# A four-network graph kernel on one core: edges taken from the highest destinations down, and two layers swept downward in blocks of 4, 4, 4 and 1

## What is computed

```
edge_index = stack([src, dst])
x = layernorm(x + L0(x, edge_index, edge_weight))   # three GCN layers with edge weights, then a linear layer
x = layernorm(x + L1(x, src, dst))                  # two SAGE layers: mean over the neighbours
x = layernorm(x + L2(x, edge_index))                # encoder, five GRU steps (segment_sum of m[src]), decoder
x = layernorm(x + L3(x, edge_index))                # one GCN layer with degree counts
# in every layer: out = segment_sum(h[src] * something, dst, num_segments=n)
```

## Time and profile before

| | us |
|---|---|
| three runs | 5507.01, 5510.14, 5510.31 (median 5510.14) |
| the profiled execution | 5502.16, its span in the trace 5500.3 |
| PE busy | 4752.6 (86%) |
| POOL busy | 2479.1 (45%), nearly all before 3043 us |
| DVE busy | 1804.3 (33%) |
| ACT busy | 1189.9 (22%) |
| read from HBM, written | 1160 MB, 240 MB |

### The profile page before, as it was taken

How to read it: one execution, slowest core, us unless ns; L and a number is a source line. 1 busy time by engine, 2 the same in 40 slices (tenths; PEclk the granted TensorE clock), 3 DMA queues, 4 the chain that set the end, 5 groups by cost and what they waited for, 6 DMA issues and landing times. The chain is left out here.

```text
span 5500.3 us, 77896 instructions
## 1 busy us (share of the span) xinstructions
PE 4752.6 (86%) x25659; PEld 2555.6 (46%) x25659; DVE 1804.3 (33%) x3215; ACT 1189.9 (22%) x2478; POOL 2479.1 (45%) x1704
## 2 busy tenths in 40 slices
PE   3544545599699999999999899899999999999999
PEld 3544544544244444444454444444444444444444
DVE  9999999900001000110050211302113021130642
ACT  4555555411011111111120101202102021120320
POOL 3888888878878888888888100000000000000000
PEclk7555555599899999999999999999999999999999
DMA  9999993399699999999989787585775857758477
GB/s 359 369 365 336 341 302 48 31 336 285 179 287 300 274 301 288 296 276 298 288 232 266 225 272 238 154 297 191 244 252 180 299 185 252 244 184 298 144 229 249
DMA packets 717098, 1402.13 MB, mean 255 GB/s; under 512 B 268372, under 2 KB 356264, under 8 KB 691880
## 3 DMA queue, kind: packets, MB, share of 16 engines
q1 hardware_dynamic: 477388, 1342.89, 73.0%
q0 software_dynamic: 225216, 0.70, 7.9%
q10 hardware_dynamic: 14364, 56.99, 2.7%
HBM read 1160.09 MB, written 240.25 MB: 255 GB/s over the span
## 5 line engine op out<-in xcount | busy, mean ns | idle before, releaser
L849 PE MATMUL psum<-arena 128*128 128x512 f16 (+3 forms) x14014 | 3666.9, 422 | 103.9 <-issue 51.9
L849 PEld LDWEIGHTS psum<-arena 128*128 (+2 forms) x14014 | 1668.2, 123 | 2040.4 <-issue 961.9
L556 POOL DMA_INDIRECT W_adj<-arena x782 | 1211.1, 1549 | 279.2 <-issue 259.8
L556 POOL DMA_INDIRECT C_adj<-arena x782 | 1213.5, 1552 | 238.4 <-issue 238.4
L711 POOL TENSOR_TENSOR arena<-arena 128x512 f32 (+1 forms) x13 | 21.5, 1651 | 1716.6 <-DVE arena L1247 1716.6
L433 DVE TENSOR_SCALAR_CACHE_REDUCE arena<-arena 128x2048 bf16<-128x2048 f32 (+7 forms) x392 | 709.4, 1875 | 0.0
L505 PE MATMUL psum<-arena 128*128 (+1 forms) x6664 | 225.0, 167 | 545.3 <-DVE arena L455 523.4
L505 PEld LDWEIGHTS psum<-arena 128*128 128x128 bf16 x6664 | 214.3, 104 | 560.4 <-issue 506.6
L1443 DVE COPY arena<-psum 128x512 f32<-128x512 f32 (+1 forms) x39 | 23.2, 653 | 1174.0 <-PE psum L867 1174.0
L273 ACT ACTIVATE arena<-arena 128x1024 bf16<-128x1024 f32 (+7 forms) x392 | 298.4, 773 | 453.0 <-DVE arena L433 439.0
L1445 DVE TENSOR_SCALAR arena<-psum,arena 128x512 f32<-128x512 f32 x30 | 21.9, 748 | 1038.9 <-PE psum L849 1038.9
(11 more groups left out here) (236 smaller groups left out, 2571.3 us busy)
## 6 DMA issues: line engine op xcount, KB each, us to landing
arena<-C_adj SPq DMA_DIRECT2D x784, 384.0 KB
arena<-W_adj SPq DMA_DIRECT2D x294, 768.0 KB
arena<-C_adj SPq DMA_DIRECT2D x392, 512.0 KB
arena<-W_adj SPq DMA_DIRECT2D x147, 1024.0 KB
arena<-C_adj SPq DMA_DIRECT2D x392, 288.0 KB
arena<-W_adj SPq DMA_DIRECT2D x147, 576.0 KB
W_adj<-arena SPq DMA_DIRECT2D x12, 6400.0 KB
W_adj<-arena SPq DMA_DIRECT2D x12, 6144.0 KB
```

The source lines that it names most:

```text
L556: return pool.indirect_dma_start(table, bass.IndirectOffsetOnAxis(idx[:, t:t + 1], 0), values[:, t:t + 1], None, compute_op=ALU.add)
L849: ins = pe.matmul(psum[:, bank + b, 0:width], lhs, ring[:, slot, b * BANK:b * BANK + width], start=begin and part == 0, stop=False, skip_g ...
```

## The change

Four things change together. `ORDER` is reversed, so that the batches of the highest destinations come first; the padding moves to the end of the first batch of the sorted list, which is now the last one taken (its edges get the weight zero and the destination 0, and DVE takes their number off node 0's degree in one more instruction). The zeros go from block 12 down to block 0, and `zones` is worked out from the lowest destination of a batch in place of the highest. The stages start and gcn 2 sweep the blocks by a new table, `DOWNWARD`; the nine other layers keep `SWEEPS`. And `needed`, from which SP's waits for the adds come, compares the highest destination of a batch with the first block of a sweep.

```diff
 ORDER = [0] + [4 * g + u for g in range((NB - 5) // 4) for u in (2, 4, 1, 3)]
 ORDER += [b for u in (0, 1) for b in range(len(ORDER) + u, NB - 1, 2)] + [NB - 1]
+ORDER = ORDER[::-1]
+PAD_EDGES = EDGES - E
+PAD_AT = B - PAD_EDGES
...
 SWEEPS = ((0, 4, 0), (4, 3, 4), (7, 3, 0), (10, 3, 4))
 SPLIT = len(SWEEPS) - 1
+DOWNWARD = ((9, 4, 0), (5, 4, 4), (1, 4, 0), (0, 1, 4))
...
-            for z in range(BLOCKS):
+            for done, z in enumerate(reversed(range(BLOCKS))):
                 at_, width = z * BANK, block_width(z)
                 for u, (c0, c1) in enumerate(halves):
-                    if z:
-                        sp.wait_ge(zeroed[u], 16 * z)
+                    if done:
+                        sp.wait_ge(zeroed[u], 16 * done)
...
-        dve.tensor_scalar(needed, limits, nearest[:, 0:1], order[:, 0:1], ALU.is_gt, ALU.mult) \
+        dve.tensor_scalar(needed, limits, farthest[:, 0:1], order[:, 0:1], ALU.is_le, ALU.mult) \
             .then_inc(s["needed_set"], 1)
-        link(dve.tensor_copy(zones, farthest))
+        link(dve.tensor_copy(zones, nearest))
         link(dve.tensor_scalar(zones, zones, 9, None, ALU.logical_shift_right))
-        dve.tensor_scalar(zones, zones, 16.0, 16.0, ALU.mult, ALU.add).then_inc(s["zones_set"], 1)
+        dve.tensor_scalar(zones, zones, -16.0, 16.0 * BLOCKS, ALU.mult, ALU.add).then_inc(s["zones_set"], 1)
...
         link(dve.tensor_copy(deg, psD[:, 0:2 * CHUNKS].rearrange("p (c k) -> p c k", c=2)))
+        link(dve.tensor_scalar(deg[0:1, 1, 0:1], deg[0:1, 1, 0:1], -float(PAD_EDGES), None, ALU.add))
...
+def sweeps_of(name, arg):
+
+    return DOWNWARD if (name, arg) in (("start", None), ("gcn", 2)) else SWEEPS
...
-            for sweep, (first, n, _) in enumerate(SWEEPS):
+            for sweep, (first, n, _) in enumerate(sweeps_of(name, arg)):
```

More of the change, by code:

```diff
@@ L312, in gpsimd @@
                   allow_small_or_imprecise_dtypes=True).then_inc(s["ramps"], 1)
-        for k, (first, n, _) in enumerate(SWEEPS[:SPLIT]):
-            pool.memset(limits[:, k:k + 1], float((first + n) * BANK)).then_inc(s["ramps"], 1)
+        for k, (first, n, _) in enumerate(DOWNWARD[:SPLIT]):
+            pool.memset(limits[:, k:k + 1], float(first * BANK)).then_inc(s["ramps"], 1)
         pool.wait_ge(s["ramps"], 7 + SPLIT)
@@ L719, in sync @@
         sp.wait_ge(ready_set, 1)
-        for k, (_, _, feeds) in enumerate(stages):
+        for k, (name, arg, feeds) in enumerate(stages):
             if feeds is None:
@@ L836, in chunk @@
             def chunk(c, slot, sweep, arrivals, begin=False, unit_of=None):
-                first, n, bank = SWEEPS[sweep]
+                first, n, bank = sweeps_of(name, arg)[sweep]
                 pe.wait_ge(landed[slot], arrivals)
@@ L998, in tensor @@
                 base.sum_dve_before, base.sum_act_before = base.sum_dve, base.sum_act
-                n = SWEEPS[sweep][1]
+                n = sweeps_of(name, arg)[sweep][1]
                 base.sum_dve += n if wide else n // 2
@@ L1148, in scalar @@
                     act.activation(abs_sb1, row["sb1"], ACT.Abs).then_inc(s["abs_set"], 1)
-                for sweep, (first, n, bank) in enumerate(SWEEPS):
+                for sweep, (first, n, bank) in enumerate(sweeps_of(name, arg)):
                     if wide and sweep:
@@ L1543, in padded @@
     def padded(v, fill):
-        v = np.concatenate([v, np.full(EDGES - E, fill, v.dtype)]).reshape(NB, B)
+        v = np.concatenate([v[:PAD_AT], np.full(PAD_EDGES, fill, v.dtype), v[PAD_AT:]]).reshape(NB, B)
         return v[ORDER].reshape(EDGES)
@@ L1561 @@
     arrays = {
-        "x": a["x"], "src": padded(a["src"], N - 1), "dst": padded(a["dst"], NP - 1),
-        "src_t": by_tile(padded(a["src"], N - 1)), "dst_t": by_tile(padded(a["dst"], NP - 1)),
+        "x": a["x"], "src": padded(a["src"], NP - 1), "dst": padded(a["dst"], 0),
+        "src_t": by_tile(padded(a["src"], NP - 1)), "dst_t": by_tile(padded(a["dst"], 0)),
         "ew_t": by_tile(padded(a["edge_weight"], 0)),
```

## The result

The changed kernel takes 5474.35 us (median of 4 executions, 5469.22 to 5476.52) against 5508.58 us before (median of 4, 5505.86 to 5510.31). The ratio is 0.9937, with a 95% interval of 0.9922 to 0.9953: 34 us faster, with the interval from 26 to 43 us. Forecast were 20 us and a time of 5490 us in a range from 5476 to 5505; the measured time lies 1.65 us under that range. The profiled execution had 5476.52 us with a span of 5474.7, 25.6 us less than the span of before.

What follows compares the result with a forecast made beforehand. POOL's chain of adds was taken to bound the kernel until 3044 us, with PE waiting. Last sweep of gcn 2 -18, POOL's end -2, ACT's copy -0.2: -20 us, from 5510.1 to 5490, range 5476 to 5505.

Steps and rivals of the forecast that it cites:

- two chains: PE's work and POOL's adds run side by side until 3044 us; PE's earlier wins are lost in gcn 2.
- the last sweep, bound by SP's issue: gcn 2's last sweep, one block: SP's load issue is slowest, 34.5 us in place of 52.5, gain 18 us.
- the rival of a slow clock: gcn 2's last sweep: PE's clock does not rise or flips, gain falls to 9.7 us, 5500; chance 0.12.
- POOL's own end: When POOL issues its last add, ahead of gcn 2's last sweep: small terms sum to -2 us.
- (a): Zeroing from block 12 down, at the start: first batches' zones ready later, delay +3 us (0 to +8).
- (b): POOL's stop at 1139 us, in the ring's first filling: from 18.00 us to near 10, -8 (-14 to +2).
- (c): Ring refilled from 256 kB to 1 MB slots after start's one-block sweep, near 1630 us: +3 (0 to +14).
- rival of a loss: Adds fall behind at the ring's refill, both waits before the C adds become 18 us; 5523 us, chance 0.05.
- the profiled execution's distance to the median carries over: Whole kernel: the profiled execution lies 8 us under the median and keeps that difference, 5482 against 5490.
- the rival that wins the whole pause: Stage start's removed pause counts in full, PE alone being the bound: 54 us and more, 5450; chance 0.02.
- The rival of a POOL that ends 14 us sooner: POOL's stop at 1139 disappears and zeroing costs nothing: 5478; chance 0.13 shared with POOL ending later.

Runs made afterwards that it cites:

- The pause put back: Changed kernel, but in stage start SP waits before the third sweep for 45 landed batches in place of 36; 5474.43 us, ratio to before 0.9942.
- the narrower first sweep: Changed kernel, but stage start sweeps blocks 10-12, 6-9, 2-5 and 0-1, so the first sweep's rows are 4.6 kB, not 6.7; 5481.59 us.

## Why the prediction was off

**Right: two chains, and POOL's is the one that counts.** The prediction said that whatever PE wins ahead of 3044 us is lost again in gcn 2. The pause put back shows it: 34.35 us more of pause, and the same time and tail to about a microsecond. Its figures along the way: third sweep of start at 1422 (1420.26), fourth at 1596 (1592.07), PE at the last sweep of gcn 2 at 2988 (2987.55), its wait 56 us (51.85).

**Right: the last sweep, bound by SP's issue.** Forecast 34.5 us from first load to last product, measured 34.0 and, in the second trace, 33.2. The forecast took 0.64 us from issue to issue and 0.15 more at each turn of the loop, 31.5 us in all; it is 0.60 and 0.28, 30.3 in all. The clock rose and stayed to the sweep's end, as taken; the rival of a slow clock is out. Behind the sweep it fell to 1.2 GHz for about 3 us in both traces of the changed kernel, and did not with the pause put back, after the same idle time of 2.10 us:

```profile
3074.00:3080.00 6.00, 3.81 (x33) 3.65 (x33) 2.26 (x7) 2.28 (x6) 0.00 (x0) 1.00 1.00 380
```

In the tail this doesn't show (2437.5 and 2435.4 against 2436.3). Against the three traces of before, 52.5, 53.6 and 53.4, the sweep's gain is 19.6 us in the mean, where 18 stood. That is 1.6 us of the miss. The whole tail fell by 21.2 us (means 2457.6 and 2436.4, the latter of the changed kernel's two traces and of the one with the pause put back), so another 1.6 us lie behind the sweep; what makes them is not shown.

**Mis-sized: POOL's own end.** This is the step that failed. The prediction gave it -2 us as the sum of three terms. Between three traces of before (mean 3048.1) and the six that have start's sweeps and loads as the changed kernel has them (3033.0 to 3042.8, mean 3037.2) it is -10.9. Term by term, by the times of single adds in those traces:
- (a) zeroing, forecast +3: the zones of the first batch came at 67.60 and DVE's indices at 70.67, as worked out; by the 337th add POOL is 2 us behind, by the 561st 1 us. Right in kind, somewhat large.
- (b) the stop at the 561st add, forecast 18 down to 10, -8: it fell from 17.8 to 19.8 us in before to 4.9 to 11 here; together with (a) POOL is 8.6 us ahead after it. (a) and (b) were forecast at -5 together: 3.6 us of the miss.
- (c) the refill of the ring, forecast +3: it went the other way. The two waits for landing took 3.50 and 4.34 us before (and up to 4.33 and 4.96 in the third trace), now 1.65 and 3.08. The rows before; then the windows ahead of the first wait, before and now, and those ahead of the second:

```profile
1604.63 0.19 POOL L531 TENSOR_TENSOR arena<-arena 128x1 f32<-128x1 f32 x1 [3.50 <-DMA C_adj<-arena]
1638.66 0.19 POOL L531 TENSOR_TENSOR arena<-arena 128x1 f32<-128x1 f32 x1 [4.34 <-DMA C_adj<-arena]
...
1590.00:1604.00 14.00, 14.00 (x59) 8.27 (x58) 1.89 (x3) 3.31 (x13) 9.30 (x7) 1.00 0.89 221
1580.00:1594.00 14.00, 14.00 (x58) 8.24 (x57) 1.66 (x3) 2.08 (x9) 11.00 (x8) 1.00 0.48 71
...
1622.00:1638.00 16.00, 16.00 (x52) 8.13 (x51) 0.00 (x0) 2.47 (x8) 10.49 (x7) 1.00 1.07 306
1612.00:1627.00 15.00, 15.00 (x36) 6.63 (x36) 0.00 (x0) 5.54 (x18) 10.63 (x7) 1.00 1.06 305
```

The prediction looked at the filling that follows the one-block sweep and gave nothing for what comes ahead of it, though its rival of a loss says that the first wait falls where traffic is light. So it does: SP fills the ring with the 256 kB chunks of the last sweep while PE still works on those of 1 MB, and 71 GB/s are moved in place of 221. The second wait comes ahead of the refill and not in it: SP loads rows of 2 kB until 1627.6, and the first load of 1 MB goes out at 1628.2. There the amount is the same, 305 against 306 GB/s, and the rows are of 2 kB in place of 4.6. Two experiments bear this out. With the pause put back the light stretch comes 35 us later, and the waits are 3.39 us beside rows of 8 kB and 2.04 in the light stretch. With the narrower first sweep both lie beside rows of 4 kB, and they are 4.08 and 4.49 us. That the width of the rows shortens the second wait is the likely reading; no run changes it alone. (c) is -3 where +3 stood: 6 us of the miss, and 12 us in all by the 815th add, of which 1 is lost again by the end.

**Wrong: that the profiled execution's distance to the median carries over.** The trace of before was an early draw, with POOL's end 6 us ahead of the other two; the changed kernel's was, at 5476.52, the latest of its four. A difference of 25.6 us between two single executions stood for one of 33 or 34 between medians. The prediction took 3044 us for POOL's end and had no spread for it, though the three times shown lay 5 to 8 us above the profiled one. Its base was also a little high: it started from a median of 5510.1 where four executions have 5508.6, and this 1.6 us is about all by which the time fell out of the range.

**The sum once more.** -21.2 (tail) - 10.9 (POOL's end) = -32 us in the traces; 5508.6 to 5474.4, -34, in the timed executions. The rest is within the spread of POOL's end, which was 10 us wide over six executions of nearly the same program. Of the 14 us that were missing, POOL's end has 9 and the tail 3. The rival that loses and the rival that wins the whole pause are both out. The rival of a POOL that ends 14 us sooner came nearest with its 5478, but not by what it named: the stop at the 561st add did not disappear, and (a) was not zero. Two readings of the prediction are off without weight: four slices of PE's row, not three, are below nine tenths, and 16.35 / 75 is 0.218, not 0.216.

## What to carry to other kernels

Where two chains meet, a pause removed ahead of the meeting is worth nothing; look for what stands behind it, and cut that to the smallest piece that can wait for the late chain. When a loop's body shrinks, ask again what binds it: here PE's 0.43 us a chunk fell below the 0.60 us that issuing a load costs. Half the loads won nothing, because the ring then turned too slowly; four chunks in one slot won back 4 to 6 us of tail. And take a second trace of a kernel before its time is split into terms of a few microseconds.

## What the runs showed of the hardware

- POOL's queue of indirect adds stops at places 112 adds apart within a table, until what is in flight is nearly through: 3 to 7 us beside the zeroing, 18 to 20 us where it met the first filling of the ring with rows of 8 kB, 8.70 us where the narrower first sweep let it meet the start of a stage, and at some of the places no stop can be seen. By the records of the queue's packets (144 an add) the adds were 7.5 behind when POOL issued its 561st in the first trace of before, and their last packet ended at 1157.8, just ahead of the next add at 1158.57; in the changed kernel they were 5.7 behind, with 1148.8 and 1149.69. Elsewhere they are 1 to 4 behind at such a place.
- From one load issued by SP in this loop to the next are 0.60 us with 131 kB a load and 0.61 with 295 kB (the first ones of the sweep in before), and 0.88 at the turn of the loop. 524 kB in one transfer, at 1 kB a row, kept PE fed at 131 kB each 0.43 us.
- PE at 2.4 GHz, busy 21.68 of 25 us with gaps of 0.2 to 0.8 us, kept its clock to the end of the sweep. Behind it, after 2.10 us of idle time, the clock fell in two traces (0.50 from 3074 to 3076 in one, from 3070 to 3073 in the other) and stayed in a third (1.00 from 3074 to 3080). The Trainium skill, TensorE: Matmul & The Clock Gate, part 1 on the clock gate, says that the clock falls after an idle window. The gaps inside the sweep agree with it; the two outcomes after the same 2.10 us show that the length of the stop alone doesn't settle it here.
